# Two transformer streams on one core: narrow attentions' keys kept as two half-zero copies, scores of 64 rows, and a new order of pieces

## What is computed

```python
x = _layernorm(x + _L0_attn_ref(x, ...))     # selective scan (Mamba), 512 channels, 16 states
x = _layernorm(x + _L0_xattn_ref(x, ctx_1024, indices, ...))   # latent attention, 16 heads of 16, 64 chosen keys a query
x = _layernorm(x + _L0_ffn_ref(x, ...))      # quantised feed-forward, 1024 wide
x = _layernorm(x + _L1_attn_ref(x, ...))     # self attention, 16 heads of 16
x = _layernorm(x + _L1_xattn_ref(x, ctx_1024, ...))            # cross attention, 16 heads of 64
x = _layernorm(x + _L1_ffn_ref(x, ...))      # mixture of 8 experts, 6 chosen, and a shared one
```

```python
energy = jnp.einsum('nhqd,nhkd->nhqk', q, k)
attention = jax.nn.softmax(energy / jnp.sqrt(jnp.float32(hd)), axis=-1)
out = jnp.einsum('nhqk,nhkd->nhqd', attention, v)
```

## Time and profile before

| | us |
|---|---|
| median of 3 runs (4187.92 to 4199.23) | 4188.95 |
| the profiled execution's own time | 4191.22 |
| its span | 4189.4 |
| PE busy (83% of the span) | 3465.2 |
| PE loading weights, beside it | 2275.8 |
| DVE busy (72%) | 3010.9 |
| ACT busy (46%) | 1908.3 |
| POOL busy (16%) | 649.4 |

### The profile page before, as it was taken

One profiled execution on the slowest core, in us unless ns is written; L12 is line 12 of the kernel. 1 busy time (PEld: TensorE's weight loads), 2 busy tenths in 40 slices (PEclk: granted clock), 3 DMA queues, 4 the chain that ended last, 5 costly groups with the idle time before them and its releaser, 6 DMA issues.

```text
span 4189.4 us, 57527 instructions
## 1 busy us (share of the span) xinstructions
PE 3465.2 (83%) x21250; PEld 2275.8 (54%) x21250; DVE 3010.9 (72%) x6490; ACT 1908.3 (46%) x4400; POOL 649.4 (16%) x516
## 2 busy tenths in 40 slices
PE   2568888898888888888888888889888888988887
PEld 1345645556565555655555564555655555564555
DVE  5677686867878687786868768686886868778622
ACT  2235445453544445444454544545454444544413
POOL 1203030210303012030210303021030301203000
PEclk8568979798887989979898897989989798997978
DMA  6425171533616144261623517152351614426010
GB/s 217 108 71 149 45 201 44 167 96 104 171 44 181 64 137 126 72 174 43 185 85 119 149 46 199 44 171 92 116 160 44 186 59 144 119 83 187 22 43 32
DMA packets 205689, 470.84 MB, mean 112 GB/s; under 512 B 23712, under 2 KB 43808, under 8 KB 190688
## 3 DMA queue, kind: packets, MB, share of 16 engines
q1 hardware_dynamic: 205408, 467.17, 37.1%
HBM read 446.11 MB, written 20.97 MB: 111 GB/s over the span
## 4 chain that ended last, share of the span: by engine, by line
PE 52%; DVE 29%; ACT 9%; issue 7%; DMA 2%; POOL 1%; SPq 0%; DVEq 0%; ACTq 0%
PE ps L632 8%; DVE region_x L1440 4%; PE ps L809 4%; PE ps L613 3%; PE ps L924 3%; PE ps L644 3%; PE ps L560 3%; PE ps L778 3%; PE ps L823 3%; PE ps L764 2%; DVE rmax L1582 2%; PE ps L863 2%; DVE nm L1477 2%; PE ps L729 2%; PE ps L790 2%
## 5 line engine op out<-in xcount | busy, mean ns | idle before, releaser
L1223 POOL TENSOR_TENSOR region_x<-region_x 128x512 f32<-128x512 f32 x512 | 649.2, 1269 | 3205.7 <-DVE region_x L1440 3205.7
L1440 DVE TENSOR_TENSOR_SCAN region_x<-ps,region_x 128x512 f32<-128x512 f32 x512 | 622.2, 1218 | 60.3 <-ACT ps L1027 59.7
L1027 ACT ACTIVATE ps<-region_x,aneg 128x255 f32<-128x255 f32 x1024 | 440.6, 470 | 454.7 <-DVE region_x L1440 400.9
L1423 DVE TENSOR_TENSOR region_x<-region_x,ps 128x512 f32<-128x512 f32 x512 | 342.3, 670 | 49.8 <-PE ps L560 23.4
L863 PE MATMUL ps<-xTy,wide 128*128 128x256 f32 x1280 | 338.9, 420 | 21.3 <-DVE region_y L1641 21.3
L1490 DVE SCALAR_TENSOR_TENSOR region_x<-region_x,cntk 128x512 f32<-128x512 f32 x256 | 167.0, 689 | 215.3 <-ACT region_x L1063 215.3
L632 PE MATMUL ps<-region_y 32*128 32x256 f32 x1024 | 254.3, 643 | 78.1 <-ACT region_y L1063 55.5
L863 PEld LDWEIGHTS ps<-xTy,wide 128*128 128x128 f32 x1280 | 258.5, 209 | 74.4 <-DVE region_y L1641 29.4
L1144 ACT ACTIVATE region_y<-ps,rmax 128x256 f32<-128x256 f32 x512 | 235.2, 480 | 84.1 <-DVE rmax L1582 84.1
L560 PE MATMUL ps<-region_x,sely 128*32 128x512 f32 x1024 | 194.1, 841 | 89.5 <-POOL region_x L1223 89.5
L632 PEld LDWEIGHTS ps<-region_y 32*128 32x128 f32 x1024 | 145.5, 307 | 211.3 <-ACT region_y L1063 164.1
(11 more groups left out here) (243 smaller groups left out, 6669.7 us busy)
## 6 DMA issues: line engine op xcount, KB each, us to landing
region_x<-rows_of_dt SPq DMA_DIRECT2D x1024, 256.0 KB, 4.7
wide<-in_wgate SPq DMA_DIRECT2D x16, 1280.0 KB, 8.0
wide<-in_wup SPq DMA_DIRECT2D x16, 1280.0 KB, 10.6
down<-in_wmoe SPq DMA_DIRECT2D x16, 1280.0 KB, 5.5
wide<-in_wq SPq DMA_DIRECT2D x16, 1024.0 KB, 4.8
wide<-in_wk SPq DMA_DIRECT2D x16, 1024.0 KB, 7.1
wide<-in_wv SPq DMA_DIRECT2D x16, 1024.0 KB, 10.0
down<-in_wo SPq DMA_DIRECT2D x16, 1024.0 KB, 8.0
```

The lines of the kernel that those rows point to most:

```text
L1027: last = f(ps[:, 1 + 2 * (k % 2), m * T + 1:(m + 1) * T], dt_rep[k % SLOTS][:, m, 1:T], ACT.Exp, scale=aneg[:, k, m:m + 1])
L1223: nc.gpsimd.tensor_tensor(hbuf[k % HSLOTS], hbuf[k % HSLOTS], csb.unsqueeze(1).to_broadcast([P, 2, T]), ALU.mult).then_inc(hc_ready, 1)
L1423: tt_(hbuf[k % HSLOTS], dtx_rep[k % SLOTS], ps[:, 2, 0:T].unsqueeze(1).to_broadcast([P, 2, T]), ALU.mult).then_inc(dbx, 1)
L1440: nc.vector.tensor_tensor_scan(flat(hbuf[k % HSLOTS]), ps[:, 1 + 2 * (k % 2), :], flat(hbuf[k % HSLOTS]), 0.0, ALU.mult, ALU.add).then_inc ...
```

## The change

Keys of both narrow attentions are written twice. Copy e holds the rows of head groups 2j + e, and zero in the others: ACT scales by a column of `pick` (1 in the kept rows, 0 in the others) or by the head mask multiplied by it, and its bias is multiplied likewise at setup. A score matmul now contracts rows 64j to 64j + 63 of the copy that keeps the wanted head: j = 0 and 1 give two heads, 2j + e, one in each half of the array. The order of heads in the maxima and in the probabilities follows. The second copy lies in parts of the regions that other tiles leave free. Setup has one more small load and six small products on DVE. The table of orders is new for PE, ACT, DVE and SP.

```diff
@@ ORDER
-    "sp": (136, "x6 y4 x5 y1 x16 y1 x44"),
-    "pe": (77, "y11 x1 y7 x1 y2 x1 y5 x1 y4 x1 y7 x1 y5 x1 y2 x1 y1 x1 y1 x1 y2 x1 y1 x1 y2 x3 y1 x2 y1 x1 y1 x3 y3 "
+    "sp": (139, "x2 y3 x1 y1 x17 y1 x5 y1 x46"),
+    "pe": (67, "x9 y3 x1 y13 x1 y2 x1 y6 x1 y4 x1 y7 x1 y4 x1 y3 x1 y5 x1 y1 x1 y1 x2 y2 x1 y2 x5 y3 x1 y1 x1 y1 x1 "
...
@@ class Attention
-                    self.QT, self.KT = place(0, (4, T)), place(1024, (4, T))
+                    self.QT, self.KT = place(0, (4, T)), (place(1024, (4, T)), place(other_keys, (4, T)))
...
-        att0 = Attention("lat", 0, True, 0, VP0, nm0, in_x)
-        att1 = Attention("self", 4, False, 1, VP1, nm1, in_y)
+        att0 = Attention("lat", 0, True, 0, VP0, nm0, in_x, 10508)
+        att1 = Attention("self", 4, False, 1, VP1, nm1, in_y, 7424)
@@ PE, narrow_attention, first pass
-                            r = slice(64 * (u % 2) + 32 * j, 64 * (u % 2) + 32 * j + 32)
-                            last = mm(ps[:, b + j, qt * T:(qt + 1) * T], a.QT[r, t, qt * P:(qt + 1) * P], a.KT[r, t, :],
+                            r = slice(64 * j, 64 * j + 64)
+                            last = mm(ps[:, b + j, qt * T:(qt + 1) * T], a.QT[r, t, qt * P:(qt + 1) * P], a.KT[u % 2][r, t, :],
                                       start=True, stop=True)
@@ second pass
-                    t, g = n // 4, n % 4
+                    t, e = n // 4, n % 4 // 2
...
-                            r = slice(32 * (g + j), 32 * (g + j) + 32)
-                            last = mm(ps[:, a.sT_bank(n + j), kt * T:(kt + 1) * T], a.KT[r, t, kt * P:(kt + 1) * P],
+                            r = slice(64 * j, 64 * j + 64)
+                            last = mm(ps[:, a.sT_bank(n + j), kt * T:(kt + 1) * T], a.KT[e][r, t, kt * P:(kt + 1) * P],
                                       a.QT[r, t, :], start=True, stop=True)
...
-                            n, h = 4 * t + g, 4 * g + t
+                            n, h = 4 * t + 2 * (g % 2) + g // 2, 4 * g + t
@@ ACT, latent
-                    last = f(att0.KT[:, t, :], bank(b)[:, t % 2, :], ACT.Identity, bias=W["aug"][:, t:t + 1])
+                    for e in range(2):
+                        last = f(att0.KT[e][:, t, :], bank(b)[:, t % 2, :], ACT.Identity, bias=augp[:, e, t:t + 1],
+                                 scale=W["pick"][:, e:e + 1])
@@ ACT, self_attention
-                    last = f(att1.KT[:, t, :], bank(6 + t // 2)[:, t % 2, :], ACT.Identity,
-                             bias=kba[:, t:t + 1], scale=W["hm1"][:, t:t + 1])
+                    for e in range(2):
+                        last = f(att1.KT[e][:, t, :], bank(6 + t // 2)[:, t % 2, :], ACT.Identity,
+                                 bias=kbp[:, e, t:t + 1], scale=hmp[:, e, t:t + 1])
@@ DVE, setup
+            for e in range(2):
+                for dst, src in ((kbp, kba), (hmp, W["hm1"]), (augp, W["aug"])):
+                    ts(dst[:, e, :], src[:], W["pick"][:, e:e + 1], None, ALU.mult).then_inc(setup_v, 1)
@@ DVE, narrow_attention
-                                col = 64 * (u % 2) + 32 * j + 16 + t
+                                col = 64 * j + 32 * (u % 2) + 16 + t
...
-                        last = nc.vector.tensor_reduce(at_nm[:, 2 * (u % 2):2 * (u % 2) + 2, :, 16 + t],
+                        last = nc.vector.tensor_reduce(at_nm[:, u % 2::2, :, 16 + t],
@@ layouts
+    pick = np.zeros((P, 2), np.float32)
+    for e in range(2):
+        for lower in (0, 64):
+            pick[lower + 32 * e:lower + 32 * e + 32, e] = 1
```

More of the change, by code:

```diff
@@ L106 @@
     ("iota", (P, 32), BF16), ("half", (P, 1), F32), ("sely", (P, 4, 32), F32),
-    ("aug", (P, 4), F32), ("qb1", (P, 4), F32), ("kb1", (P, 4), F32), ("hm1", (P, 4), F32),
+    ("aug", (P, 4), F32), ("pick", (P, 2), F32), ("qb1", (P, 4), F32), ("kb1", (P, 4), F32), ("hm1", (P, 4), F32),
     ("wout", (P, M, D), F32),
@@ L116 @@
 ]
-FIRST = 20
+FIRST = 21
 def build(nc, dram, out):
@@ L164, in build @@
         kba = sb("kba", (P, 4))
+        kbp, hmp, augp = sb("kbp", (P, 2, 4)), sb("hmp", (P, 2, 4)), sb("augp", (P, 2, 4))
         qbh = sb("qbh", (P, 4))
@@ L270, in build, with __init__ @@
         class Attention:
-            def __init__(self, tag, base, masked=False, first_pair=0, VP=None, NM=None, place=None):
+            def __init__(self, tag, base, masked=False, first_pair=0, VP=None, NM=None, place=None, other_keys=0):
                 self.base, self.masked, self.first_pair = base, masked, first_pair
@@ L1259, in _ @@
             tt_(kba[:], kba[:], W["aug"][:], ALU.add).then_inc(setup_v, 1)
+            v.wait_ge(setup_v, n + 4)
+            for e in range(2):
+                for dst, src in ((kbp, kba), (hmp, W["hm1"]), (augp, W["aug"])):
+                    ts(dst[:, e, :], src[:], W["pick"][:, e:e + 1], None, ALU.mult).then_inc(setup_v, 1)
+            n += 6
             for buf, value in ((VP0, 1.0), (VP1, 1.0), (nm0, 0.0), (nm1, 0.0), (shiftb, 0.0), (wsplit, 0.0)):
@@ L1749, in layouts @@
         "half": np.repeat(np.float32([0, 16]), SEL).reshape(P, 1), "ones": np.ones((P, P), np.float32), "tri": tri,
-        "aug": aug, "selx": selx.astype(bf), "sely": sely,
+        "aug": aug, "pick": pick, "selx": selx.astype(bf), "sely": sely,
         "wq0": tiles(heads16(n["L0_xattn_W_q"].T)), "wdown0": tiles(n["L0_xattn_W_kv_down"].T),
```

## The result

The changed kernel takes **3948.6 us** (median of 4 runs, 3947.62 to 3951.12) against 4188.43 us for the kernel before on the same chip (4185.15 to 4199.23): ratio 0.942, 95% interval 0.9407 to 0.9442. That is 240 us less. The forecast was 4085 us, from 4010 to 4200: the direction was right, the gain was more than twice what I gave and lies outside the range, beyond the rival "more than I take" (4016).

What follows compares the result with a forecast made beforehand. No single engine was taken to bind (chain: PE 52%, DVE 29%). The terms summed to −7.0 us a period, −105 over 15 periods, so 4189 became 4084, stated as 4085 us; range 4010 to 4200.

Steps and rivals of the forecast that it cites:

- more than I take: Feed-forward stage hides L924 down to +4, self attention and projections lose 8: −11.5 us a period, 4016 us; chance 0.14.
- L924 leaves the head: Head: y's second transposition no longer stands behind the MoE's down projection; minus 9.4 us a period.
- L924 into the feed-forward stage: Feed-forward: L924 fits PE's free time, but x's late norm and first quantisation enter where DVE leads; plus 5.5 us.
- gives all back: Feed-forward: L924 or x's late norm lengthens the DVE-bound stage by the full 9.4; −3.1 us a period, 4142 us; chance 0.2.
- Self attention: Self attention and following projections: score units mostly at the higher clock, four scans moved into the projections; minus 5 us.
- term 5: Score units: two 32-row units in unlike row groups ran at once, 64-row ones cannot; about twice a period, plus 1 us.
- second rival: Self attention and projections: DVE or row transfers hold the stage, idle time replaces the clock's gain; −1.0 a period, 4174 us; chance 0.12.
- Keys twice: Self attention: PE's scores wait for four more key copies per batch on ACT, plus 1.9 us; nothing in latent attention.
- term 6: Latent attention: score units at 2.01 us in a short low-clock stretch near 1404 speed up; minus 1 us.

Runs made afterwards that it cites:

- second undo run: Changed kernel with y's down projection and late norm back in the head, key-count copy behind y's norm and query scaling on DVE: 4127.4 us.

## Why the prediction was wrong, and where it was right

The direction, and the ground for it (that 64-row records hold the clock up where 32-row ones do not), held; 320 us hang on it. By its terms:

1. *L924 leaves the head*: forecast −9.4. With 32 rows and one copy of the keys the head went from 31.8 to 19.9, −11.9. The cause was right and the size 2.5 too small: behind the late L458, L729 had also waited 0.8 us longer and taken 1.7 us longer for the same 16 records. The first line is of before, the second of the changed kernel:

```profile
1277.93 5.39 PE L729 MATMUL ps<-xTy,wq 128*128 128x256 f32 x16 [1.46 <-ACT xTy L968]
1201.95 3.72 PE L730 MATMUL ps<-xTy,wq 128*128 128x256 f32 x16 [0.69 <-ACT xTy L969]
```

2. *L924 into the feed-forward stage*: forecast +5.5; FF went from 53.5 to 60.0, +6.5. The size was near and the cause half: L925 costs nothing there (it fills PE's 12.76 us wait). What is left for the 6.5 is DVE's norm, which the forecast named, and L675. My rival "gives all back" is excluded by the second undo run.
3. *Self attention*: by the marks of the table the price of the copies lies in the head, so −5 and the +1 of term 5 stand against this: −4 forecast, and −0.7 measured (85.5 to 84.8). The clock rose as forecast, from 0.65 and 0.62 to 0.82 and 0.89, but most of the gain went into the order: the rows took 12.2 us off the new order, which alone had made the region 11.5 longer. The stage also took in 3 us of cross scores (22 of 64 records of L791) that had stood in the latent stage. DVE was busy 79.4 of the 86.9 us of a window over it, and waited 46 us for row transfers over the whole span. That was the second rival's mechanism; it held this stage and not the kernel.
4. *Keys twice*: forecast +1.9. In the new order with 32 rows the head takes 21.7 us with two copies and 19.9 with one, +1.8, with a wait of 1.83 us for L1115 as described. It comes back in the first pass: head and first pass together take 43.3 with two and 43.1 with one.
5. *Lost concurrency*: forecast +1. The two units of the latent pass that stand together show it, first with 32 rows, then with 64:

```profile
1424.39 1.16 PE L614 MATMUL ps<-region_x 32*128 32x256 f32 x16
1427.45 1.13 PE L614 MATMUL ps<-region_x 32*128 32x256 f32 x8 [1.90 <-DVE nm L1482]
...
1318.12 1.89 PE L614 MATMUL ps<-region_x 64*128 64x256 f32 x16
1321.28 1.13 PE L614 MATMUL ps<-region_x 64*128 64x256 f32 x8 [1.26 <-DVE nm L1482]
```

The two take 0.7 us longer, but PE then waits less for DVE's maximum, and the next unit starts 3.16 us after the first where it was 3.06: +0.1. In self attention two units take 2.11 and 3.79 us, and the next one starts 7.1 us behind the first unit in both kernels. The Trainium skill (TensorEngine Tiling (Array Packing), "Theoretical Speedup") promises most to small contractions; here the packing of 32-row units was worth about 0.1 us a period where it can be seen, and their clock cost 320 / 15 = 21.
6. **The step that failed: term 6, the latent attention at "minus 1 for it".** I had taken the stretch from 1373.5 to 1451.3 as a PE at full clock with fixed work, and priced one low unit near 1404; the work that the order moves out of it I had put at nothing, without a reason, although term 2 itself names L674's move. It gave −10.7 us. In one pair of windows (77.77 and 66.97 us) the difference is made up so: 5.7 us of PE work moved out of the stretch (3.0 of L790, 2.7 of L674, L667 and L778, by the groups of the two windows); of the rest, L809's mean went from 451 to 388 ns, which is 2 us, other PE groups gave another 2, and waits 1.2. Of that work L674 went into the feed-forward stage, so part of this −10.7 and of the +6.5 of term 2 is one move; both stages together went −4.2 where I had +4.5. The mean clock of 0.96 hid a stretch at 0.84:

```profile
1390.69:1411.85 21.16, 16.95 (x118) 10.20 (x117) 18.92 (x92) 11.26 (x44) 0.00 (x0) 0.84 0.39 142
```

Above all I summed the parts as if they were independent. The new order makes the latent first pass dense, among cross scores of 64 rows. Of that stage I asked only what the clock costs in the *old* order (about 1 us: 77.6 to 76.8 with 64 rows), and not what 32-row records would do in the *new* one: 77.7 us, against 66.9 with 64. The order takes work out of the stage and the rows let it keep the clock; the rows alone give 0.8 us there and the order alone nothing.

The whole period was forecast at −7.0 and measured at −15.2. Terms 1 to 5 sum to −6.0 as forecast, and to −4.5 as measured (−10.3, +6.5 and −0.7). That they come so near is in part luck: the head gave 2.8 us more than terms 1 and 4, and self attention 3.3 less than terms 3 and 5. The other 9.7 us a period (146 us) are term 6.

## To carry to other kernels

Before pricing a clock or an overlap from the old trace, lay the new order beside it and price the work in the place where it will stand: two changes that each look small, or even lose, can hold each other up. If records with few rows stand in dense PE code, zero-padded operands that fill more rows can pay by the clock of everything around them (320 us here), and a run that changes only the row slice measures that cleanly. To find where an instruction costs nothing, look for PE's longest wait in a stage that another engine binds: here 12.76 us took in a down projection that had cost 8.9 us in the head.

## What the runs showed of the hardware that I had not expected

- Row counts act on the clock of their neighbours. With 146 or 147 records of the same work, the stretch of the latent first pass was granted 0.61 with 32-row scores (busy 91%) and 1.00 with 64-row scores (busy 88%), although the added rows hold only zeros in the keys, and L810 of the other stream took 537 ns instead of 388 over the latent stage.
- Where more of the 128-row work (L824, L845) and the products with the values (L645) stood among them, 32-row scores kept the clock at 1.00 (lat 2, 30.4 of 30.9 us busy). Scores of the same shape cost 10 us a period in one neighbourhood and 1 in another. Which of the neighbours holds the clock there was not tested.
- 64 rows are no guarantee: after PE's waits of 4.49 and 1.36 us between the passes, 64-row pairs took 2.08 us for the first 7.6 us of the second pass, and again after a wait of 3.14 us later in it (clock 0.74 over the pass, against 0.89 without the added scans).
